# Queries, row maxima and stored heads on one PSUM bank: moving the transposes to other units of the attention

## The chip, the cores and the metric

One Trainium2 chip, one core. The metric is the device time of one execution in microseconds (us), lower is better. The engines are TensorE (PE), VectorE (DVE), ScalarE (ACT), GpSimd (POOL) and SyncE (SP, which here only issues DMAs).

## The reference

A block of three parts over 2 x 1024 tokens of width 512, each with a residual: half a mixture-of-experts FFN, attention, half the same FFN again.

```python
x = x + 0.5 * ffn(layernorm(x))      # 2 shared experts, 8 routed ones of width 352, top 2
x = x + attn(layernorm(x))
x = x + 0.5 * ffn(layernorm(x))

def attn(x):                          # 16 heads of 32, 4 key/value heads, 1024 tokens a batch
    q, k, v = x @ Wq.T, x @ Wk.T, x @ Wv.T
    q, k = rope(q), rope(k)
    attn = softmax(q @ k.T * scaling)  # no mask
    return (attn @ v) @ Wo.T
```

The change touches the attention alone.

## The kernel before

`order_of_work` writes one list of items, and each engine's program walks through the same list and does its part of every item in that order; semaphores hold between the engines. So an item's place in the list is its place in every engine's queue.

**Projections.** The 16 tiles of 128 tokens are projected in the order `PROJECTED` (batch 1 first, then batch 0), one tile for each `i`, in four parts `("project", t, 0..3)`: keys and values in parts 0 and 1, queries in parts 2 and 3, into two PSUM banks (0 and 1, or 2 and 3, in turn). VectorE and GpSimd rotate the result (`rotary`, L1766 and L1768). After four tiles the turned keys (`turn_keys`, L1262, bank 6) are split into a high part by ScalarE (L1521, `early_hi`) and a low part by VectorE (L1847, `early_lo`), and SP places them with twelve DMAs into `KS` (L1046). Queries of the first two of the eight groups (a group is one key head of one batch with its four query heads) are turned in bank 7 (`MISC`; `turn_queries`, L1272) at the tiles named by `EARLY_QUERIES`, split into the same `early_hi` (L1526) and `early_lo` (L1854), and placed by twelve DMAs into `QS` (L1056). The two buffers exist once: `split_before` makes each split wait for the DMAs of the one before.

The softmax is done with the row maximum folded into the contraction: `row_max` (L1292) multiplies a tile of 128 queries with all 1024 keys into a pair of PSUM banks, VectorE takes the negated maximum (L1859, `nmf_first` or `nmf_later`), and when a head's eight are there `place_max` turns them in `MISC` (L1300), ScalarE and VectorE split them (L1535, L1865, `place_low`), and SP writes them as two rows of `QS`. The 32 maxima of the first group stand beside the projections of the tiles `i` = 9 to 15, and use one pair of banks (4 and 5), so each matmul pair waits for the reduction before it.

**Heads.** Each group has 32 units: head `h`, half `hf` of the queries, and pair of key tiles (`pair`, 0 to 3). `un` is the unit within its group. A unit `u` has on TensorE the scores (L1310, two matmuls), half of the values of unit `u - 5` (L1325, L1326), a row maximum of the next group, and the other half of the values, eight matmuls; three pairs of banks go round. ScalarE takes the exponential (L1547, `PT`) and most high parts (L1556, `Ph`), VectorE the others (L1878); the low parts `Pl` are on GpSimd (L2017) or VectorE (L1886). Of 16 units VectorE casts 3 and subtracts 5, GpSimd subtracts 11. After each fourth unit ScalarE copies the output (L1564, `OT`), and at pair 1 `store_head` turns it in `MISC` (L1336) and VectorE normalises it with four small instructions (L1786 to L1793), the last of which, `qtok`, frees `MISC`. At `un` 5 and 21 `turn_queries` turns half of the queries of the group after next, also in `MISC`, after `store_head` of the same unit; at pair 2 of every eighth unit `place_max` uses it too.

Of the kernel before, what the change touches and what calls it, by code (L numbers as in the profile page):

```python
# [35 lines left out]
REP = NH // NKV  # L36
QT = S // P
# [139 lines left out]
UNITS = 2 * REP * (QT // 2)  # L177


def unit(u):  # L180

    n, un = divmod(u, UNITS)
    return n, un // QT, un // (QT // 2) % 2, un % (QT // 2)
# [10 lines left out]
def lo_on_vector(u):  # L194
    return u % 4 != 0 if in_last_group(u) else u % 16 in (2, 4, 8, 10, 14)
# [15 lines left out]

QUERY_STACK, KEY_STACK = (0, 1, 0), (0, 0, 1)

EARLY_QUERIES = {5: (0, 0), 9: (0, 1), 10: (1, 0), 12: (1, 1)}


def out_bank(n, hf):
# [13 lines left out]
def order_of_work():  # L231
# [131 lines left out]
    maxima = [("row_max", 0, h, t) for t in range(QT) for h in range(REP)]  # L363

    def beside_step():
        for item in beside.pop(0) if beside else ():
            work.append(item)
            if item[0] == "norm" and item[3] == 2 + TPG:
                normed.add(item[2])

    for i, t in enumerate(PROJECTED):
        if i > 0:
            beside_step()
        tq = i - QT
        if i == QT:
            work.append(("ones",))
        if tq == 0:
            work.append(("queries_start",))
        while t // TPG not in normed:
            beside_step()  # L380
        work.append(("project", t, 0))
        if tq == 0:

            work.extend([("turn_keys", PROJECTED[i - 1]), ("place_keys", ORDER[1])])
        for h in range(REP - 1):
            if tq > 0:
                work.append(maxima.pop(0))
                if h == 2 and tq <= REP:

                    work.append(maxima.pop(0))  # L390
            if h == 1:
                beside_step()
                if i in EARLY_QUERIES:
                    work.append(("turn_queries", *EARLY_QUERIES[i]))
            work.append(("project", t, h + 1))
            if i in EARLY_QUERIES and h == 1:
                work.append(("place_queries", *EARLY_QUERIES[i]))
            if i == NT - 1 and h == REP - 2:
                for h2 in range(2):
                    work.extend([("place_max", 0, h2), ("place_low", 0, h2)])  # L400
            if i > 0 and tq != 0 and h == 1:
                work.append(("turn_keys", PROJECTED[i - 1]))
                if i % TPG == 0:
                    work.append(("place_keys", PROJECTED[i - 1] // TPG))
        if tq > 0:
            work.append(maxima.pop(0))
    work.extend([("turn_keys", PROJECTED[-1]), ("place_keys", PROJECTED[-1] // TPG)])
    for h in range(2, REP):
# [3 lines left out]
    in_flight, outputs, maxima, lows = [], [], [], []  # L412
    groups = len(KV_GROUPS)
    for u in range(groups * UNITS):
        n, h, hf, pair = unit(u)
        un = u % UNITS
        if u and un == 0 and n == groups - 1:
            work.append(("spare_bank",))
        if in_flight:
            work.append(("split_hi", in_flight[-1]))  # L420
            if not lo_on_vector(in_flight[-1]):
                work.append(("split_lo", in_flight[-1]))
        work.append(("scores", u))
        in_flight.append(u)
        if lows:
            work.append(("place_low", *lows.pop(0)))
        w = in_flight[0] if in_flight[0] == u - LAG else None

        between = w is not None and unit(w)[3] > 0 and n + 1 < groups
        if between:  # L430
            work.append(("half_values", w, 0))
        if n + 1 < groups:
            work.append(("row_max", n + 1, un // QT, un % QT))
        if maxima and pair == 2:
            lows.append(maxima.pop(0))
            work.append(("place_max", *lows[-1]))
        if n + 1 < groups and un % QT == QT - 1:
            maxima.append((n + 1, un // QT))
        if len(in_flight) > 1 and lo_on_vector(in_flight[-2]):
            work.append(("split_lo", in_flight[-2]))  # L440
        if w is not None:
            in_flight.pop(0)
            work.append(("half_values", w, 1) if between else ("values", w))
            if unit(w)[3] == QT // 2 - 1:
                outputs.append(unit(w)[:3])
        if outputs and pair == 1:
            work.append(("store_head", *outputs.pop(0)))
        if n + 2 < groups and un % (UNITS // 2) == 5:
            work.append(("turn_queries", n + 2, un // (UNITS // 2)))
        if n + 2 < groups and un % (UNITS // 2) == 6:  # L450
            work.append(("place_queries", n + 2, un // (UNITS // 2)))
        if n == groups - 1 and un % QT == 0:
            work.append(("wo", un // QT))
# [30 lines left out]
def macaron(nc, ctx, x, ffn_w, gate_w, wqkv, wo, rope, ident, triones, rconst, out):  # L484
# [202 lines left out]
    o_done, o_added = signal("o_done"), signal("o_added")  # L687

    work = order_of_work()
    dispatch_place = {t: i for i, t in enumerate(t for g in ORDER for t in group_tiles(g))}  # L690
    combines = [tuple(key) for kind, *key in work if kind == "combine"]
# [1434 lines left out]
```

## Time and profile before

| | |
|---|---|
| median of 3 runs | 1828.98 us (1827.82 to 1831.81) |
| the profiled execution | 1831.98 us, its span 1830.2 us |
| mean granted clock of TensorE | 0.968 |
| projections beside the first row maxima | about 587 to 672 us |
| heads | about 674 to 1272 us |

The span is the time from the first to the last instruction. A granted clock of 1.00 is 2.4 GHz, and the lower level is 1.2 GHz, so that a stretch at 0.86 had both.

### The profile page before, as it was taken

What the parts mean: (1) busy time and instruction counts of PE and PEld (TensorE: products, weight loads), DVE (VectorE), ACT (ScalarE), POOL (GpSimd) and SP (SyncE); (2) the same over time, 40 slices, a digit from 0 to 9 for tenths busy, and PEclk for the clock granted to TensorE, in tenths of its full rate; (3) what the DMA queues carried; (4) which work ended last, traced back from release to release, by engine and by line L of the source; (5) the groups of instructions that cost most, each with busy time, mean ns of one, the idle gap of its engine ahead of it and who ended that gap; (6) DMA issues with size and microseconds to landing.
All of it is one profiled execution on the core that took longest, in us unless ns stands there. A gap on an engine that the chain in (4) does not pass through costs nothing.

```text
span 1830.2 us, 24612 instructions
## 1 busy us (share of the span) xinstructions
PE 1661.1 (91%) x8356; PEld 1328.8 (73%) x8356; DVE 1068.1 (58%) x1786; ACT 828.1 (45%) x1148; POOL 938.5 (51%) x681
## 2 busy tenths in 40 slices
PE   6999999999976578888888888887999999999997
PEld 5888898998865455555555555554888889989985
DVE  4454322222685578999989999898645432222226
ACT  4322232232322028888888888875333122323221
POOL 3115673336533127778777887763030619550746
PEclk9999999999988889999999999999989999999998
DMA  9215543333722210100011000001210535432427
GB/s 346 78 41 199 210 179 123 125 130 113 224 93 55 53 32 19 35 19 18 19 27 27 18 18 18 1 24 48 94 52 1 215 118 200 165 131 73 177 81 241
DMA packets 65829, 175.73 MB, mean 96 GB/s; under 512 B 10544, under 2 KB 11440, under 8 KB 63152
## 3 DMA queue, kind: packets, MB, share of 16 engines
q1 hardware_dynamic: 52880, 100.48, 16.8%
q0 software_dynamic: 12832, 73.67, 11.4%
q8 instruction: 75, 1.23, 0.3%
q14 instruction: 42, 0.34, 0.1%
HBM read 102.29 MB, written 55.84 MB: 86 GB/s over the span
## 4 chain that ended last, share of the span: by engine, by line
PE 52%; DVE 28%; issue 10%; DMA 6%; ACT 2%; SPq 1%; POOL 1%; DVEq 0%; POOLq 0%; ACTq 0%
PE PS L1095 9%; PE PS L1097 9%; PE PS L1096 9%; DVE nmf_later L1859 6%; DVE Pl L1886 6%; DVE Ph L1878 5%; DVE nmf_first L1859 3%; DMA xs<-x_routed 2%; DMA xn<-x_routed 2%; PE PS L1217 2%; PE PS L1292 2%; PE PS L1222 2%; PE PS L1220 2%; PE PS L1219 2%; PE PS L1218 2%
## 5 line engine op out<-in xcount | busy, mean ns | idle before, releaser
L2017 POOL TENSOR_TENSOR Pl<-PT,Ph 128x1024 fp32r<-128x1024 f32 x162 | 429.4, 2666 | 150.0 <-ACT Ph L1556 118.4
L1547 ACT ACTIVATE PT<-PS 128x1024 f32<-128x1024 f32 x256 | 258.9, 1016 | 65.0 <-PE PS L1310 53.0
L1325 PE MATMUL PS<-Ph,V 128*65 128x512 f32 x512 | 208.5, 407 | 11.3 <-DVE Pl L1886 10.2
L1556 ACT ACTIVATE Ph<-PT 128x1024 fp32r<-128x1024 f32 x198 | 208.8, 1054 | 3.1
L1859 DVE TENSOR_REDUCE nmf_later<-PS 128x1 f32<-128x1024 f32 x160 | 190.1, 1212 | 32.8 <-PE PS L1292 32.5
L1326 PE MATMUL PS<-Pl,V 128*65 128x512 f32 x512 | 203.5, 397 | 0.0
L1292 PE MATMUL PS<-KS,QS 96*128 96x512 f32 x512 | 170.0, 414 | 32.2 <-DVE nmf_first L1859 25.1
L1935 POOL TENSOR_TENSOR W<-raw,W 128x544 fp32r<-128x544 f32 x144 | 190.2, 1356 | 1.5
L1310 PE MATMUL PS<-QS,KS 98*128 98x512 f32 x512 | 174.8, 423 | 16.7 <-DVE nmf_later L1859 12.2
L1826 DVE TENSOR_TENSOR thid<-thid,PS 128x352 f32<-128x352 f32 x78 | 40.7, 521 | 245.8 <-ACT thid L1491 245.8
L1491 ACT ACTIVATE thid<-PS 128x352 f32<-128x352 f32 x78 | 36.3, 465 | 260.3 <-PE PS L1222 260.3
L1095 PE MATMUL PS<-xh,W 128*128 128x512 f32 x352 | 146.3, 416 | 3.2 <-DVE xl L1579 1.6
L1292 PEld LDWEIGHTS PS<-KS,QS 96*128 96x128 f32 x512 | 97.6, 196 | 70.1 <-DVE nmf_first L1859 32.0
L1096 PE MATMUL PS<-xl,W 128*128 128x512 f32 x352 | 142.5, 405 | 0.0
L1097 PE MATMUL PS<-xh,W 128*128 128x512 f32 x352 | 142.5, 405 | 0.0
L1923 POOL DMA_DIRECT2D raw<-ffn_w x18 | 10.0, 556 | 257.9 <-POOLq L1921 193.6
L1859 DVE TENSOR_REDUCE nmf_first<-PS 128x1 f32<-128x1024 f32 x96 | 115.1, 1215 | 36.3 <-PE PS L1292 36.1
L1310 PEld LDWEIGHTS PS<-QS,KS 98*128 98x128 f32 x512 | 91.2, 195 | 58.4 <-DVE nmf_later L1859 23.4
L1886 DVE TENSOR_TENSOR Pl<-PT,Ph 128x1024 fp32r<-128x1024 f32 x94 | 128.3, 1371 | 0.6
L1964 POOL DMA_INDIRECT x_routed<-xq,pos x64 | 64.8, 1013 | 122.2 <-issue 117.1
L1830 DVE TENSOR_TENSOR htl<-PS,hth 128x384 fp32r<-128x384 f32 x78 | 43.5, 558 | 138.8 <-ACT hth L1497 138.8
L1951 POOL TENSOR_TENSOR W<-raw,W 128x512 fp32r<-128x512 f32 (+1 forms) x36 | 43.6, 1240 | 137.2 <-ACT W L1455 137.2
(183 smaller groups left out, 4050.9 us busy)
## 6 DMA issues: line engine op xcount, KB each, us to landing
raw<-ffn_w POOLq DMA_DIRECT2D x18, 2176.0 KB, 10.4
y_routed<-ytile SPq DMA_DIRECT2D x78, 256.0 KB, 2.0
xn<-x_routed SPq DMA_DIRECT2D x40, 256.0 KB, 3.0
x_routed<-xq SPq DMA_DIRECT2D x1, 9984.0 KB, 28.8
xs<-x_routed SPq DMA_DIRECT2D x38, 256.0 KB, 3.2
QS<-later_hi SPq DMA_DIRECT2D x96, 64.0 KB, 2.0
raw<-ffn_w SPq DMA_DIRECT2D x6, 768.0 KB, 9.8
raw<-ffn_w SPq DMA_DIRECT2D x2, 2176.0 KB, 9.2
```

The costliest lines, as they stand in the source:

```text
L1095: e.matmul(dst, lh, rh, start=first, stop=False)
L1096: e.matmul(dst, lh, rl, start=False, stop=False)
L1097: return e.matmul(dst, ll, rh, start=False, stop=end)
L1292: mm = e.matmul(PS[:, i + hf, :], QS[n % 3][0:STK, h, t * P:(t + 1) * P], KS[0:STK, b, g, hf * GRP:(hf + 1) * GRP], start=True, stop=True)
L1310: mm = e.matmul(PS[:, i + j, :], KS[0:ROWS, b, g, kt * P:(kt + 1) * P], QS[n % 3][0:ROWS, h, hf * GRP:(hf + 1) * GRP], start=True, stop=True)
L1325: e.matmul(PS[0:VCOL, ob, :], V[:, b * QT + kt, g, :], high_part(u)[:, js], start=kt == 0, stop=False)
L1326: mm = e.matmul(PS[0:VCOL, ob, :], V[:, b * QT + kt, g, :], low_part(u)[:, js], start=False, stop=kt == QT - 1)
L1547: e.activation(PT[:, u % PTBUF, :], PS[:, i:i + 2, :].rearrange("p b n -> p (b n)"), ACT.Exp, scale=SCALE).then_inc(p_ready.sem, 1)
L1556: e.activation(high_part(u)[:], PT[:, u % PTBUF, :], ACT.Copy).then_inc(ph_act.sem, 1)
L1859: e.tensor_reduce(row_maxima(n)[:, h, t:t + 1], PS[:, i:i + 2, :].rearrange("p b n -> p (b n)"), AX.X, ALU.max, negate=True).then_inc(max_ ...
L1886: e.tensor_tensor(low_part(u)[:], PT[:, u % PTBUF, :], high_part(u)[:], ALU.subtract).then_inc(pl_dve.sem, 1)
L2017: e.tensor_tensor(low_part(u)[:], PT[:, u % PTBUF, :], high_part(u)[:], ALU.subtract).then_inc(pl_pool.sem, 1)
```

## The change

Three numbers in the heads, and two in the projections. The queries of the groups from the third on are turned at `un` 6 and 22 (and split and placed at 7 and 23) instead of 5 and 21 (6 and 22). The row maxima are turned at pair 3 instead of pair 2. In the projections the last two of the four early query halves go from the tiles `i` = 10 and 12 to 11 and 14; the first row maximum stands ahead of part 3 of tile `i` = 9 instead of ahead of part 1, so tile 9 has two instead of five, and the tiles 10, 11 and 12 have six instead of five.

```diff
-EARLY_QUERIES = {5: (0, 0), 9: (0, 1), 10: (1, 0), 12: (1, 1)}
+EARLY_QUERIES = {5: (0, 0), 9: (0, 1), 11: (1, 0), 14: (1, 1)}
+
+FIRST_MAXIMA = QT + 1
...
         for h in range(REP - 1):
-            if tq > 0:
+            if i > FIRST_MAXIMA or i == FIRST_MAXIMA and h == 2:
                 work.append(maxima.pop(0))
-                if h == 2 and tq <= REP:
+                if h % 2 == 0 and FIRST_MAXIMA < i <= FIRST_MAXIMA + 3:
 
                     work.append(maxima.pop(0))
...
-        if tq > 0:
+        if i >= FIRST_MAXIMA:
             work.append(maxima.pop(0))
...
-        if maxima and pair == 2:
+        if maxima and pair == 3:
             lows.append(maxima.pop(0))
             work.append(("place_max", *lows[-1]))
...
-        if n + 2 < groups and un % (UNITS // 2) == 5:
+        if n + 2 < groups and un % (UNITS // 2) == 6:
             work.append(("turn_queries", n + 2, un // (UNITS // 2)))
-        if n + 2 < groups and un % (UNITS // 2) == 6:
+        if n + 2 < groups and un % (UNITS // 2) == 7:
             work.append(("place_queries", n + 2, un // (UNITS // 2)))
```

## Rows read from the trace of the kernel before

**Rows 1.** The page, part 1: busy us, share of span, instructions, by engine.

```profile
PE 1661.1 (91%) x8356; PEld 1328.8 (73%) x8356; DVE 1068.1 (58%) x1786; ACT 828.1 (45%) x1148; POOL 938.5 (51%) x681
```

**Rows 2.** VectorE in order of time, projections: start, length, what [idle before].

```profile
591.66 0.69 DVE L1854 TENSOR_TENSOR early_lo<-PS,early_hi 128x512 fp32r<-128x512 f32 x1 [0.26 <-ACT early_hi L1526]
...
617.08 1.23 DVE L1859 TENSOR_REDUCE nmf_first<-PS 128x1 f32<-128x1024 f32 x1 [1.88 <-PE PS L1292]
...
654.95 1.22 DVE L1859 TENSOR_REDUCE nmf_first<-PS 128x1 f32<-128x1024 f32 x1 [0.83 <-PE PS L1292]
...
656.99 1.23 DVE L1859 TENSOR_REDUCE nmf_first<-PS 128x1 f32<-128x1024 f32 x1 [0.23 <-PE PS L1292]
```

**Rows 3.** Windows by tile: length, then busy us (instructions) by engine, clock, DMA.

```profile
587.60:598.30 10.70, 9.35 (x38) 7.11 (x36) 7.45 (x10) 0.88 (x2) 0.45 (x1) 0.78 0.20 48
598.30:609.40 11.10, 8.07 (x41) 5.99 (x39) 8.47 (x12) 0.88 (x2) 1.72 (x2) 1.00 0.26 64
609.40:621.70 12.30, 9.26 (x37) 6.69 (x36) 7.97 (x11) 0.28 (x1) 1.72 (x2) 0.86 0.12 30
621.70:644.20 22.50, 9.80 (x40) 7.49 (x39) 9.13 (x14) 1.48 (x3) 1.72 (x2) 0.77 0.24 58
644.20:652.90 8.70, 7.12 (x36) 5.38 (x34) 6.67 (x10) 0.28 (x1) 1.72 (x2) 1.00 0.13 32
...
661.60:671.40 9.80, 6.63 (x32) 4.68 (x30) 7.12 (x12) 0.81 (x3) 2.65 (x3) 1.00 0.00 0
```

**Rows 4.** Waits, 575 to 680 us: who waits <- for whom: total, times, longest.

```profile
ACT early_hi L1521 <- DMA QS<-early_hi: 9.8, 1, 9.8
...
PE PS L1292 <- DMA KS<-early_lo: 6.3, 1, 6.3
```

**Rows 5.** Windows, half a group of the heads each, groups 3 and 6 (counted from 0).

```profile
901.30:938.90 37.60, 32.61 (x152) 21.79 (x151) 34.23 (x44) 31.67 (x37) 29.15 (x12) 1.00 0.09 22
...
1126.90:1164.00 37.10, 33.83 (x148) 22.33 (x147) 34.46 (x43) 31.30 (x36) 29.02 (x12) 0.95 0.01 2
```

**Rows 6.** VectorE in order of time, heads of group 3.

```profile
916.65 1.23 DVE L1859 TENSOR_REDUCE nmf_later<-PS 128x1 f32<-128x1024 f32 x1 [2.16 <-PE PS L1292]
...
927.91 1.23 DVE L1859 TENSOR_REDUCE nmf_later<-PS 128x1 f32<-128x1024 f32 x1 [0.90 <-PE PS L1292]
```

**Rows 7.** TensorE in order of time, heads of group 3.

```profile
911.63 0.41 PE L1336 MATMUL PS<-identf,OT 65*128 65x65 f32 x4
914.55 0.66 PE L1272 MATMUL PS<-identf,qtok 128*128 128x128 f32 x4 [2.50 <-DVE qtok L1793]
...
925.74 0.27 PE L1300 MATMUL PS<-identf,nmf_later 128*8 128x128 f32 x1 [1.39 <-DVE qtok L1793]
```

**Rows 8.** Waits in the heads, 690 to 1130 us.

```profile
PE PS L1272 <- DVE qtok L1793: 27.6, 11, 2.5
...
PE PS L1300 <- DVE qtok L1793: 15.9, 12, 1.4
```

**Rows 9.** ScalarE in order of time, tile twelve.

```profile
626.25 0.60 ACT L1526 ACTIVATE early_hi<-PS 128x512 fp32r<-128x512 f32 x1 [1.49 <-PE PS L1272]
636.66 0.60 ACT L1521 ACTIVATE early_hi<-PS 128x512 fp32r<-128x512 f32 x1 [9.81 <-DMA QS<-early_hi]
```

**Rows 10.** The chain that ended last, in order of time: start, length, what.

```profile
634.59 1.99 DMA QS<-early_hi
```

**Rows 11.** By source line: count, ns min/median/max (casts, VectorE's and GpSimd's low parts).

```profile
L1878 DVE CAST Ph<-PT x58: 676/2070/2901, 680.2 to 1268.1; 128x1024 fp32r<-128x1024 f32 x58
L1886 DVE TENSOR_TENSOR Pl<-PT,Ph x94: 1202/1224/3404, 684.1 to 1268.8; 128x1024 fp32r<-128x1024 f32 x94
L2017 POOL TENSOR_TENSOR Pl<-PT,Ph x162: 2356/2407/3444, 679.0 to 1259.8; 128x1024 fp32r<-128x1024 f32 x162
```

**Rows 12.** VectorE in order of time, heads of group 6.

```profile
1152.58 1.23 DVE L1859 TENSOR_REDUCE nmf_later<-PS 128x1 f32<-128x1024 f32 x1 [2.37 <-PE PS L1292]
1153.72 3.02 DVE L1886 TENSOR_TENSOR Pl<-PT,Ph 128x1024 fp32r<-128x1024 f32 x1
```

## Prediction

> **What bounds the kernel now.** I read first the page's shares [rows 1]: TensorE is busy 91% of the span and VectorE 58%, but these are means over stages. The change touches two stages only, so I asked for each what its row maxima wait for: the projections from tile nine on (about 587 to 672 us), and the heads (about 674 to 1272 us).
>
> In the projections each of the 32 row maxima of the first group goes through one pair of PSUM banks: two matmuls, VectorE's reduction, then the next two matmuls. Two reductions in a row start 2.04 us apart [rows 2] (654.95 to 656.99) even with half a projection's matmuls between them, so TensorE's projection work is hidden there and the chain of 32 maxima sets the end. Stretches cut at the last reduction of each projected tile [rows 3] show: with four maxima a tile takes 8.7 us, with five 11.1 us, the last tile 9.8 us (it also turns two rows of maxima). One tile takes 22.5 us. The waits [rows 4] say why: ScalarE stood 9.8 us before the keys' high part until a DMA out of `early_hi` had landed. Turned queries and turned keys share `early_hi` and `early_lo`; in this tile both are placed, back to back. The same waits show 6.3 us in which TensorE stood before the first maximum until the keys' last DMA had landed.
>
> In the heads I looked at VectorE's order of time over half a group (16 units of group 3, counted from 0). It is busy 34.23 of 37.6 us, TensorE 32.61, ScalarE 31.67 [rows 5]: VectorE is nearly gapless, so it is the bound, and what is worth anything is its own idle time. There are two gaps of note, 2.16 and 0.90 us before a row maximum [rows 6], 3.06 us together. Both follow a TensorE wait for bank MISC [rows 7]: turning the queries comes right after turning a stored head (911.63) and waits 2.50 us for VectorE's last read of that head; the transposed maxima wait 1.39 us for the same. The waits over the steady part [rows 8] count 11 of the one and 12 of the other.
>
> **The change, part by part.** No instruction is added or removed; all are moved.
>
> *Tile nine's first maxima.* Before, TensorE stood at the first maximum with three quarters of the tile still to project. Now the second and third part and the first group's second query half come first. The keys land when they did, so the first reduction stays at 587.6 us or so; ScalarE's copy of the queries' high part must wait for the same landing (it overwrites `early_hi`), and VectorE's low part, with the first reduction queued behind it, ends 1.3 us after it by 0.60 us [rows 9] and 0.69 us [rows 2], also at about 587.6. So nothing is gained or lost at the start; the work moved into the wait is work the chain would have hidden anyway.
>
> *The chain from there.* Before: 10.7 + 11.1 + 12.3 + 22.5 + 8.7 + 8.7 + 9.8 = 83.8 us, by tile [rows 3]. After, tile nine has two maxima, the next three have six each, the last three four. First pitch: 3.1 us, that of a pair with half a projection between at the low clock (at 617.08, 1.88 of idle behind a reduction of 1.22 [rows 2]), as TensorE has just stood still. A tile of four costs 8.7 = 4 x 2.04 + 0.55; one of six 6 x 2.04 + 0.55 = 12.8, three of them 38.4. Turning queries adds about 0.35 (11.1 less 5 x 2.04 + 0.55), and falls on tiles 11 and 14, placing the keys in tile 12 about 0.3 (between 0 and VectorE's 0.69). The last three: 8.7 + 8.7 + 9.8 = 27.2. Sum 3.1 + 38.4 + 0.35 + 0.3 + 0.35 + 27.2 = 69.7. One spell at the low clock such as tile 11 had (12.3 against 10.75 for five maxima without turning) adds 1.5: 71.2. **First term: 83.8 - 71.2 = 12.6 us.** Bounds: 14.1 without that spell; -0.9 if the three tiles of six run wholly at 1.2 GHz (below).
>
> Does the 9.8 us wait return elsewhere? From one high part to the free buffer took 10.4 us (626.25 to 636.66 [rows 9]): SP issues twelve transfers, and the last one landed 1.99 us after its issue began [rows 10]. Queries of tile 11 and keys of tile 12 are now 12.8 us apart, queries of tile 14 and the last keys some 13 us (8.7 plus most of a tile). Both clear it by about 2.4 us. The queries' second half of group 1 is first read at the fifth unit of the heads, long after its landing.
>
> *The heads: maxima turned one unit later.* TensorE then reaches the transpose about 1.9 us later (eight matmuls of a unit, out of 152 in 32.61 us [rows 5]), after the 1.39 us are over. The gap of 0.90 goes. Their first reader is the next group or the eighth unit on, so lateness costs nothing; behind it on ScalarE stand the next exponential and high part, which no longer wait for the transpose.
>
> *The queries turned one unit later.* TensorE now does unit six's matmuls (1.9 us) in the 2.50 us, then still waits for the same VectorE read until 914.55, turns, and delivers the next maximum 2.1 us later, at 916.65 as before. VectorE meanwhile has one reduction it did not have, 1.23 us [rows 6]. So 2.16 - 1.23 = 0.93 us of idle is left and 1.23 saved. Together 2.13 us of 3.06.
>
> *What the saved idle time meets.* VectorE's casts took 0.68 to 2.90 us and its subtractions 1.20 to 3.40 [rows 11]: the long ones wait behind a GpSimd subtraction. Group 6, which turns no queries, shows it: VectorE busy 34.46 of 37.1 us though 0.68 us of work is gone (with 34.23 before), 0.91 us more waiting, one subtraction of 3.02 us among it [rows 12]. I take 0.3 of the 0.91, as the new order keeps more slack than that group's: 1.8 us per half group. 11 x 1.8 = 19.8; the first half, with no wait at its queries, 0.9; group 6's two halves lose a gap of 2.37 us each [rows 12], less 0.3: 4.1. **Second term: 24.8 us.** Bounds: 11 x 3.06 + 0.9 + 4.7 = 39; and about 8 (rival B).
>
> The Trainium skill (SBUF — State Buffer, section on the two separate sides) says that VectorE and GpSimd take a shared pair of ports as an exclusive lock, held for a whole instruction, for VectorE operations with two SBUF inputs or a two-port mode. The trace agrees: the shortest cast is 0.68 us and the median 2.07.
>
> The profiled execution took 1832.0 us, 3.0 more than the median 1829.0. 1832.0 - 12.6 - 24.8 = 1794.6, so against the median **1792 us**.
>
> **Rivals.** *A, the forecast:* both terms, 1785 to 1800.
>
> *B, the ports are the bound.* By the shortest durations [rows 11] a half group holds 3 x 0.68 + 5 x 1.20 + 11 x 2.36 = 34.0 us of work that excludes one another. If this can't be packed closer than in group 6 (37.1 us without any turning, only 0.4 to 0.5 us shorter than the others), a half group gains 0.5: 11 x 0.5 + 2.5 = 8 us. Then 1829 - 12.6 - 8 = 1808. For it: group 6. Against: that half had a low clock (0.95) and the 1.7 us wait for MISC that the change removes.
>
> *C, the clock.* Granted clock 0.86 in tile 11, which had no long wait, 0.77 in tiles 9 and 12 [rows 3]. Tiles of six maxima give TensorE less to do per us than those of five. At 1.2 GHz two pitches a tile grow by 1.1 (3.1 against 2.04) to 1.5 and the others by about 0.5: 5 us a tile, 15 for three, so the first term is -0.9 and the time 1829 + 0.9 - 24.8 = 1805.
>
> *D, slower.* The clock in the heads: over a half group TensorE's 32.6 us would be about 65 at 1.2 GHz, 29 more than 36. From 37/29 = 1.3 half groups (some 85 us at the low clock) on, the whole gain is gone; at three, 1829 + 50 = 1879. For it: a drop in group 6 (0.95). Against: 1.00 over the steady half, with both waits in it, and the change takes waits away.
>
> *E, all gaps close:* 39 + 14.1 = 53, 1776 us.
>
> **How the numbers follow.** A 0.59, B 0.19, C 0.11, E 0.06, D 0.03, and 0.02 that a wait I don't see cancels it all. A alone: 1785 to 1800. B and C lie at 1808 and 1805, so the range runs from 1781 to 1812 and leaves out E, D and the edges of B. A measurement tells about 0.2% (3.7 us) from no change: faster 0.95, within it 0.02, slower 0.03.
>
> **What would show it.** The last reduction before the heads near 659 instead of 671.5; no 9.8 us wait at the keys' high part; one tile no longer at 22.5 us but three at about 12.8. In the heads, TensorE's wait before the queries' turning 0.6 us instead of 2.5, none before the maxima, a VectorE gap near 0.9 after the queries, half groups of 35.8 us. Wrong if ScalarE waits for a landing at the keys of tile 12 or at the end, if casts and subtractions on VectorE grow, or if the clock row falls.

## The result, and the profile of the changed kernel

| | before | changed |
|---|---|---|
| median of four runs each, one chip (us) | 1830.39 (1827.82 to 1835.89) | 1779.12 (1774.1 to 1787.51) |
| profiled execution: time; span (us) | 1832.0; 1830.2 | 1774.1; 1772.3 |

The ratio is 0.9721, 95% interval [0.9676, 0.9765]: 51 us gained where 37 were forecast, and 1779.1 lies 2 us below the range. The sign was right, both mechanisms were at work, and the second term was far too small.

The page first, part 1 (busy us, share of the span, instructions), against [rows 1]: the counts are the same, VectorE is busy 12.4 us less, GpSimd 8.5 us less. No instruction was removed, so some instructions became shorter.

```profile
PE 1659.6 (94%) x8356; PEld 1327.1 (75%) x8356; DVE 1055.7 (60%) x1786; ACT 824.1 (46%) x1148; POOL 930.0 (52%) x681
```

**The projections.** Stretches of the changed kernel cut at the last reduction of each tile, as in [rows 3]; the first window runs from the first to the second reduction (length, busy us of PE, PEld, DVE, ACT and POOL, granted clock, DMA share, GB/s):

```profile
588.12:591.88 3.76, 3.76 (x11) 2.98 (x11) 2.43 (x4) 0.00 (x0) 0.00 (x0) 0.50 0.29 70
591.88:605.57 13.69, 10.47 (x42) 7.59 (x40) 9.23 (x12) 0.28 (x1) 1.76 (x2) 0.85 0.16 40
605.57:619.70 14.13, 10.23 (x43) 7.48 (x41) 10.01 (x13) 0.88 (x2) 1.72 (x2) 0.88 0.13 33
619.70:634.10 14.40, 9.87 (x39) 7.06 (x37) 9.83 (x14) 0.88 (x2) 1.71 (x2) 0.88 0.20 48
634.10:642.84 8.74, 6.99 (x35) 5.30 (x33) 6.69 (x11) 0.28 (x1) 1.72 (x2) 1.00 0.21 51
642.84:651.90 9.06, 7.34 (x39) 5.69 (x37) 7.28 (x11) 0.88 (x2) 1.72 (x2) 1.00 0.09 23
651.90:661.76 9.86, 6.67 (x32) 4.68 (x30) 7.16 (x12) 0.81 (x3) 2.69 (x3) 1.00 0.24 59
```

The tile of 22.5 us is gone. The chain from first to last reduction takes 73.64 us where it took 83.8: 10.2 us gained, against 12.6 in the first term. It starts at 588.12, where 587.6 was forecast. This is one trace. Eleven kernels of the experiments have the same projections, and in the twelve traces together the chain takes 73.5 to 73.7 us seven times (mean granted clock of that stretch 0.90) and 74.9, 75.7, 77.5, 77.5 and 79.9 us in the others (0.92, 0.86, 0.84, 0.84 and 0.82). The old order takes 83.6 to 84.3 us in five traces (0.86 to 0.89), so the change of order is worth 4 to 10 us there, and most of the spread goes with the clock. ScalarE's high parts in order of time show where the 9.81 us of [rows 9] went: nowhere. They stand 15.2 us apart, and the keys' (628.22) waits for TensorE, not for a DMA. The queries' of tile 14 (647.36) and the last keys' (661.83) stand 14.5 us apart and wait for TensorE too.

```profile
586.84 0.60 ACT L1528 ACTIVATE early_hi<-PS 128x512 fp32r<-128x512 f32 x1 [5.18 <-DMA KS<-early_lo]
613.05 0.60 ACT L1528 ACTIVATE early_hi<-PS 128x512 fp32r<-128x512 f32 x1 [1.95 <-PE PS L1274]
628.22 0.60 ACT L1523 ACTIVATE early_hi<-PS 128x512 fp32r<-128x512 f32 x1 [2.61 <-PE PS L1264]
```

**The heads.** From the last reduction of the projections to the last of the heads the changed kernel takes 484.1 us (661.76 to 1145.9), the kernel before 527.3 (671.45 to 1198.8): 43.2 us gained, against 24.8 in the second term. Two half groups, a steady one and one of group 6, to be held against [rows 5]:

```profile
735.95:770.36 34.41, 32.77 (x151) 21.64 (x150) 33.11 (x44) 31.37 (x37) 28.35 (x12) 1.00 0.10 24
1080.15:1114.26 34.11, 32.50 (x148) 21.32 (x147) 33.84 (x43) 30.90 (x36) 29.93 (x12) 1.00 0.01 2
```

A steady half group fell from 37.6 to 34.4 us, 3.2 us, where 1.8 were forecast. The idle time of VectorE fell from 3.37 (37.60 less 34.23) to 1.30, by 2.07; the forecast had 2.13. But its busy time, with the same instructions, fell too, from 34.23 to 33.11, by 1.1 us, where a growth of 0.3 had been put in. VectorE in order of time in that half group shows the rest:

```profile
738.99 2.08 DVE L1880 CAST Ph<-PT 128x1024 fp32r<-128x1024 f32 x1
...
749.04 1.21 DVE L1861 TENSOR_REDUCE nmf_later<-PS 128x1 f32<-128x1024 f32 x1
751.28 1.22 DVE L1861 TENSOR_REDUCE nmf_later<-PS 128x1 f32<-128x1024 f32 x1 [1.03 <-PE PS L1294]
752.42 0.68 DVE L1856 TENSOR_TENSOR later_lo<-PS,later_hi 128x512 fp32r<-128x512 f32 x1
753.02 0.68 DVE L1880 CAST Ph<-PT 128x1024 fp32r<-128x1024 f32 x1
...
765.02 1.75 DVE L1880 CAST Ph<-PT 128x1024 fp32r<-128x1024 f32 x1
```

There is one gap, 1.03 us behind the queries' turning (0.93 forecast), and none behind the maxima. The three casts of a half group take 2.08, 0.68 and 1.75 us, 4.51 together; before they took 2.09, 1.55 and 2.07 (904.49, 919.65 and 933.37 us of its trace), 5.71. Casts are one size, 0.68 us at the shortest [rows 11], so the rest is waiting, and these 1.2 us are the fall in busy time. GpSimd in order of time shows behind what (2.36 us is the shortest of its subtractions): the first cast starts while the second of a pair is under way, which ends at 740.52, and ends 0.55 us after it; the second cast falls between two of them, and the later one waits for it.

```profile
734.77 5.75 POOL L2019 TENSOR_TENSOR Pl<-PT,Ph 128x1024 fp32r<-128x1024 f32 x2
...
748.03 4.77 POOL L2019 TENSOR_TENSOR Pl<-PT,Ph 128x1024 fp32r<-128x1024 f32 x2 [1.17 <-ACT Ph L1558]
753.78 2.41 POOL L2019 TENSOR_TENSOR Pl<-PT,Ph 128x1024 fp32r<-128x1024 f32 x1 [0.98 <-DVE Ph L1880]
```

The same in VectorE's groups by line, of the changed kernel and then of the one before:

```profile
L1880 DVE CAST Ph<-PT 128x1024 fp32r<-128x1024 f32 x58 | 91.0, 1570 | 0.0
```

```profile
L1878 DVE CAST Ph<-PT 128x1024 fp32r<-128x1024 f32 x58 | 101.1, 1743 | 0.0
```

TensorE now waits 0.77 us before it turns the queries (0.6 forecast; [rows 7] had 2.50), and the waits from 680 to 1100 us hold eleven of these (second line below) and none before the maxima, where [rows 8] had twelve:

```profile
DVE nmf_later L1861 <- PE PS L1294: 8.5, 9, 1.1
PE PS L1274 <- DVE qtok L1795: 8.3, 11, 0.8
```

**The sum.** The spans differ by 57.9 us: 10.2 in the projections, 43.2 in the heads, 5.0 after the last reduction, less 0.5 because the chain began later. Of what comes after the last reduction the change moves only the last turning of maxima. That part takes 626.4 us here and 631.5 in the kernel before, and from 626.4 to 634.5 in the traces of all kernels of this document, so the 5.0 us are a part of this pair of executions, not of the change (the medians differ by 51).

### The profile page after: what moved, and what is told of

It reads as the page before. It is cut to its first block, busy times and chain, and to the rows that moved or that the text cites. A ratio compares the mean times of both kernels' runs of the same rounds, so it can differ in the third digit from the quotient of the medians.

```text
span 1772.3 us, 24612 instructions
## 1 busy us (share of the span) xinstructions
PE 1659.6 (94%) x8356; PEld 1327.1 (75%) x8356; DVE 1055.7 (60%) x1786; ACT 824.1 (46%) x1148; POOL 930.0 (52%) x681
## 4 chain that ended last, share of the span: by engine, by line
PE 56%; DVE 26%; DMA 7%; issue 6%; ACT 3%; SPq 1%; POOL 0%; DVEq 0%; ACTq 0%; POOLq 0%
PE PS L1097 10%; PE PS L1099 10%; PE PS L1098 10%; DVE nmf_later L1861 6%; DVE Pl L1888 5%; DVE Ph L1880 4%; DVE nmf_first L1861 4%; PE PS L1219 2%; DMA xn<-x_routed 2%; PE PS L1224 2%; PE PS L1222 2%; PE PS L1221 2%; PE PS L1223 2%; PE PS L1220 2%; PE PS L1294 2%
## 5 line engine op out<-in xcount | busy, mean ns | idle before, releaser
L2019 POOL TENSOR_TENSOR Pl<-PT,Ph 128x1024 fp32r<-128x1024 f32 x162 | 422.5, 2625 | 111.7 <-ACT Ph L1558 81.3
```

The source lines that it names most:

```text
L2019: e.tensor_tensor(low_part(u)[:], PT[:, u % PTBUF, :], high_part(u)[:], ALU.subtract).then_inc(pl_pool.sem, 1)
```

## The experiments

All kernels here, the control included, have two more register operations than the changed kernel (a shifted value and a clamped one are kept in registers of their own). `changed` is the changed kernel with nothing else: 1783.17 us (1775.84 to 1789.58), ratio 0.9733 [0.9704, 0.9761], half groups 34.43 us. Ratios are to the kernel before on the same chip, in five rounds; `low_four`, `casts_two`, `before_low_four` and the three `pe_` kernels had three.

### One part of the change at a time

The kernel before with one part each. `proj_only` has the first three pieces of the diff, with `QT + 1` written out for `FIRST_MAXIMA`; of these only the first is shown:

```
-EARLY_QUERIES = {5: (0, 0), 9: (0, 1), 10: (1, 0), 12: (1, 1)}
+EARLY_QUERIES = {5: (0, 0), 9: (0, 1), 11: (1, 0), 14: (1, 1)}
```

`maxima_only` has the first line below, `queries_only` the other two, `heads_only` all three:

```
-        if maxima and pair == 2:
+        if maxima and pair == 3:
-        if n + 2 < groups and un % (UNITS // 2) == 5:    (turn_queries)
+        if n + 2 < groups and un % (UNITS // 2) == 6:
-        if n + 2 < groups and un % (UNITS // 2) == 6:    (place_queries)
+        if n + 2 < groups and un % (UNITS // 2) == 7:
```

> The kernel before with the projections' part of the change alone: early queries at tiles 11 and 14, the first row maximum ahead of part 3 of tile nine, six maxima in tiles 10 to 12; the heads stay as before. Theory: the stretch from the first to the last reduction goes from 83.8 to 73.6 us as in the changed kernel, and nothing else moves: 10 us less in all, ratio 0.9945, half groups in the heads still 37.6 us. Rival: the heads' half groups lock into another pattern with another start, and the time is off the 10 us by more than 5 in either direction.

> The kernel before with the heads' part of the change alone (queries turned at units 6 and 22, maxima at pair 3); the projections stay as before, with the 9.8 us wait. Theory: half groups of 34.4 us instead of 37.6, the heads some 42 us shorter, ratio 0.977. Rival: the shorter half group needs the start that the new projections give, and the half groups are at 35.5 us or more here, 25 us less in all.

> The kernel before with the queries turned one unit later and nothing else; the maxima are still turned at pair 2. Theory: of the changed kernel's 3.2 us a half group, 1.1 come from VectorE's idle time at the queries, and 1.1 from waits behind GpSimd which the new place of the cast after the queries saves; both belong to this move: half groups of 35.4 us, some 25 us less in all, ratio 0.986, the shortest of the three casts near 0.68 us. Rival: the fall of the GpSimd waits belongs to the maxima's move or to both together: half groups of 36.5 us, 13 us less.

> The kernel before with the maxima turned at pair 3 instead of 2 and nothing else; the queries stay at units 5 and 21. Theory: only the 0.9 us gap of VectorE goes, half groups of 36.7 us, and group 6 loses its two gaps of 2.4 us: 10 plus 5, some 15 us less, ratio 0.992. Rival (the GpSimd waits fall here): half groups of 35.6 us, some 28 us less. Second rival (VectorE's waits behind GpSimd take the place of the gap): half groups still 37.6 us and 5 us less.

| kernel | median us | ratio | projections us | steady half group us |
|---|---|---|---|---|
| before, here | 1832.91 | | 83.8 | 37.60 |
| proj_only | 1829.62 | 0.9978 [0.9961, 0.9994] | 73.7 | 37.6 |
| heads_only | 1789.20 | 0.9752 [0.973, 0.9774] | 84.1 | 34.43 |
| queries_only | 1806.25 | 0.9843 [0.9819, 0.9867] | 84.3 | 35.46 |
| maxima_only | 1823.12 | 0.9941 [0.9919, 0.9964] | 83.6 | 37.65 |

`heads_only` gains 43.7 us, which is what the heads gave in the changed kernel's trace. From the last reduction of the projections to the last of the heads its trace has 484.1 us, as the changed kernel's, `queries_only` 500.7, `maxima_only` 519.6 and the kernel before 527.3.

In `queries_only` a half group takes 35.46 us, in `maxima_only` 37.63; a window of each, from cast to cast:

```profile
908.93:944.39 35.46, 32.60 (x152) 21.60 (x151) 33.25 (x44) 31.71 (x37) 28.92 (x11) 1.00 0.10 24
```

```profile
920.04:957.67 37.63, 34.11 (x151) 22.99 (x151) 33.25 (x45) 31.30 (x37) 28.17 (x12) 0.95 0.09 22
```

VectorE is busy 33.25 us in both, a good 1.0 us less than before, and the two moves together give 1.1. But they shorten different casts. The three of a half group take 2.08, 1.55 and 2.07 us before, 2.07, 0.68 and 2.08 in `queries_only`, 2.08, 0.68 to 0.98 and 1.55 in `maxima_only`, and 2.08, 0.68 and 1.75 in the changed kernel. So the queries' move frees the second cast and the maxima's move shortens the third. That the second is short in `maxima_only` too comes with the long gaps told below and needs no move: in the kernel before the only cast behind a long gap takes 0.94 us where the others take 1.53 to 1.58, and in `before_low_four` the ten behind long gaps take 0.68 to 1.00, the one behind a gap of 2.15 takes 1.56. First a long gap and the cast behind it in the kernel before, then the short gap of `before_low_four` and its cast:

```profile
729.27 1.23 DVE L1859 TENSOR_REDUCE nmf_later<-PS 128x1 f32<-128x1024 f32 x1 [3.61 <-PE PS L1292]
...
732.27 0.94 DVE L1878 CAST Ph<-PT 128x1024 fp32r<-128x1024 f32 x1
```

```profile
918.55 1.23 DVE L1860 TENSOR_REDUCE nmf_later<-PS 128x1 f32<-128x1024 f32 x1 [2.15 <-PE PS L1292]
...
921.55 1.56 DVE L1879 CAST Ph<-PT 128x1024 fp32r<-128x1024 f32 x1
```

What also differs is the clock. In `maxima_only` TensorE's wait before the queries is 2.67 us, and the granted clock behind it is low for a few microseconds, so that the turning takes 1.11 us instead of 0.66 and VectorE's gap is 3.66 instead of 2.16. Of that kernel, TensorE and VectorE in order of time:

```profile
951.05 1.11 PE L1272 MATMUL PS<-identf,qtok 128*128 128x128 f32 x4 [2.67 <-DVE qtok L1794]
...
954.66 1.23 DVE L1860 TENSOR_REDUCE nmf_later<-PS 128x1 f32<-128x1024 f32 x1 [3.66 <-PE PS L1292]
```

and windows of it around this place:

```profile
940.00:950.00 10.00, 7.75 (x36) 4.98 (x34) 9.93 (x14) 8.63 (x10) 8.20 (x4) 1.00 0.00 1
950.00:960.00 10.00, 8.95 (x34) 6.42 (x35) 6.11 (x11) 5.66 (x7) 6.05 (x3) 0.83 0.11 26
960.00:970.00 10.00, 9.77 (x49) 6.50 (x47) 9.64 (x15) 9.73 (x13) 6.93 (x4) 1.00 0.23 55
```

All eleven of its gaps behind the queries are of this kind, 3.2 to 3.7 us, about 1.4 more than 2.15. A spell costs less than that where the cast behind it is spared: two half groups of the kernel before with one spell take 76.0 us where two others take 75.2, and four of `proj_only` with three spells 154.4 where 150.4 would be usual. At 0.8 to 1.3 us each eleven spells are an estimated 9 to 15 us, so the maxima's move alone may well have shortened the work, and the spells have taken it back; no half group of `maxima_only` without a spell is there to show it. The length of the wait does not decide alone: behind waits of 2.5 us the kernel before has one long gap of eleven, `proj_only` three. This also tells where `proj_only`'s gain went in part. Its projections are shorter by 10 us, and its heads took 530.4 us instead of 527.3, two spells more. In its profiled execution the span is 8.2 us shorter than before (1822.0 against 1830.2), in the medians 3.3; its twelve executions have mean clocks of 0.958 to 0.969, and more such spells in those not profiled would account for the rest, which no trace here shows.

So the parts are not additive: alone the heads' two moves gain 26.7 and 9.8 us in the medians, together 43.7. The intervals are some 4 us wide to each side, so the medians alone would leave this open; the traces of the heads say it more sharply, with 26.6 and 7.7 us against 43.2. With a wait of 0.6 (`queries_only`) or 0.77 us (changed kernel) no gap of that kind is left in either trace.

### The projections: which move removes the wait

`undo_first` is the changed kernel with the first maxima in their old places, `undo_early` the one with the early queries back at tiles 10 and 12.

> The changed kernel with the first row maxima back at part 1 of tile nine and five in tiles 9 to 12, the early queries still at tiles 11 and 14. Theory: the early queries' move alone takes away the 9.8 us wait, the chain of 32 maxima is as long either way: first to last reduction 74 to 76 us against 73.6, up to 2 us more in all (TensorE's work at the low clock in tile nine). Rival: the maxima's move is what gives the queries of tile 11 and the keys of tile 12 their room: with tiles of 11.1 us instead of 12.8 ScalarE waits for a landing there, and the stretch is 80 us.

> The changed kernel with the early queries turned at their old tiles (10 and 12) and the first maxima at their new ones. By the wait theory the 9.8 us wait of ScalarE for the landing of the queries' copies is back before the keys' high part, projections of 83 us instead of 75, time 1788. Rival (the order of the maxima alone spares the wait): 1779.

`undo_first`: 1778.47 us, 0.9694 [0.9669, 0.9719], projections 74.8 us. `undo_early`: 1789.36 us, 0.9772 [0.9754, 0.979], projections 87.1 us, and the wait is back, as ScalarE's last row in tile twelve shows:

```profile
634.34 0.60 ACT L1522 ACTIVATE early_hi<-PS 128x512 fp32r<-128x512 f32 x1 [9.74 <-DMA QS<-early_hi]
```

The early queries' move carries the whole gain of the projections. With the first maxima's move alone they take 3 us longer in the one trace (87.1 against 83.8), at a granted clock of 0.82 where the kernel before had 0.89, so the clock may be the reason. Beside the other, with 73.5 to 79.9 us in the traces of the changed order and 74.8 here, its worth can't be told from nothing.

### The heads: gap against wait

`cast_6` moves a cast of VectorE from unit 7 to 6 of 16, `queries_78` turns and places the queries one unit later still (7 and 8).

> The changed kernel with VectorE's cast of unit 7 given to ScalarE and that of unit 6 to VectorE; the queries stay at units 6 and 7. Theory (the extra gain over the forecast is that the cast after the queries falls into GpSimd's gap): the cast now stands ahead of the turned queries' low part, GpSimd is in a subtraction then, the cast takes 1.5 to 2.1 us again, and half groups grow from 34.4 to 35.2 us or more, some 10 us in all. Rival (VectorE's waits behind GpSimd are the same in sum wherever the casts stand, and it was the shorter idle time alone): half groups stay at 34.4 us within 0.2.

> The changed kernel with the queries turned one unit later again (units 7 and 23, placed at 8 and 24). Theory: TensorE's last wait for the bank (0.77 us) and VectorE's gap of 1.0 us behind it go; with the waits behind GpSimd as they are, half groups of 33.4 us and 12 us less than the changed kernel. Rival: the cast after the queries leaves GpSimd's gap, 1.1 us come back, and the time is that of the changed kernel or 3 us more. Second rival: the next stored head, at unit 9, now waits for the queries' low part, and the wait has only moved.

`cast_6`: 1778.26 us, 0.9702 [0.9677, 0.9726], half groups 34.25 us. `queries_78`: 1785.12 us, 0.9747 [0.9719, 0.9775], half groups 34.55. A half group of each:

```profile
920.00:954.25 34.25, 32.69 (x152) 21.65 (x151) 33.19 (x44) 30.95 (x37) 28.20 (x11) 1.00 0.10 24
```

```profile
957.00:991.55 34.55, 32.68 (x152) 21.71 (x151) 34.28 (x44) 31.42 (x37) 29.52 (x12) 1.00 0.10 24
```

In `cast_6` the theory that a moved cast would meet a subtraction and cost 0.8 us or more misses: its three casts take 2.08, 0.81 and 1.55 us, 4.44 together as in the changed kernel (4.51), and its rival (the same sum of waits, the same length within 0.2 us) holds. `queries_78` is the telling one. VectorE has no gap of note left and is busy 34.28 us of 34.55, 1.2 more than in the changed kernel, with casts of 2.08, 2.08 and 1.90. Yet a half group is longer by only 0.1 us: the idle time has become waiting behind GpSimd, and TensorE's next stored head waits in its turn. VectorE, then TensorE, in order of time:

```profile
991.61 2.09 DVE L1881 CAST Ph<-PT 128x1024 fp32r<-128x1024 f32 x1
...
995.48 0.46 PE L1338 MATMUL PS<-identf,OT 65*128 65x65 f32 x4 [0.73 <-DVE later_lo L1857]
```

While VectorE stands for TensorE, GpSimd gets on with its subtraction, and the cast behind the gap no longer meets it: here a gap of VectorE and a wait behind GpSimd trade one for the other. What then keeps the length near 34.4 us is not shown by either kernel.

### What bounds a half group now

My next theory was that the ports which the two engines share are the bound: 34.0 us by rival B's sum, against 34.1 to 34.55 in all these kernels. Four kernels change where casts and subtractions run, the last beside the old order:

```
low_six          u % 16 in (2, 4, 8, 10, 12, 14)   subtractions on VectorE, before: (2, 4, 8, 10, 14)
low_four         u % 16 in (2, 4, 8, 14)
casts_two        u % 16 in (1, 13)                 casts on VectorE, before: (1, 7, 13)
before_low_four  low_four's edit in the kernel before
```

> The changed kernel with VectorE doing six low parts of 16 units instead of five (unit 12 too), GpSimd ten. Theory (port theory: after the change a half group is bound by what VectorE and GpSimd can't do at once, 3 x 0.68 + 5 x 1.20 + 11 x 2.36 = 34.0 us, and only 0.4 us of 34.4 are free of it): the sum is now 32.8, VectorE's own work 31.5, so half groups shrink to 33.2 us, some 16 us less than the changed kernel. Rival (VectorE theory: VectorE's own work and its gaps are the bound, the waits behind GpSimd are an accident of phase): half groups grow by about 1 us to 35.4 us.

> The changed kernel with four low parts on VectorE instead of five (unit 10 goes to GpSimd, which has twelve). Port theory: 3 x 0.68 + 4 x 1.20 + 12 x 2.36 = 35.2 us, half groups of 35.4 us, 14 us more than the changed kernel. VectorE theory: VectorE has 1.1 us less to do, half groups of 33.3 to 34.4 us.

> The changed kernel with two casts on VectorE instead of three; the high part of unit 7 goes to ScalarE. Port theory: 34.0 less 0.68 is 33.3 us, half groups of 33.7 us if ScalarE (31.3 us busy, 32.4 then) keeps up, 10 us less. VectorE theory: VectorE loses 0.68 us of work, and half groups the same 0.7 us; the two theories differ in the 1.7 to 2.1 us that the other casts take: they stay so long by the port theory, and by the other they may fall. Rival: ScalarE, now with an exponential and a high part in three units in a row, becomes late and half groups are 34.4 us or more.

> The kernel before with four low parts on VectorE instead of five (unit 10 goes to GpSimd). Port theory: before the change the 34.0 us of exclusive work left 3.6 of 37.6 us free, so 1.2 more fits: half groups stay within 0.5 of 37.6 us, or shrink since VectorE has 1.1 us less to do, and what costs 14 us after the change costs nothing before it. Rival: it costs the same before as after, 1 us a half group and 14 us in all, and the port was the bound of both.

Medians and ratios: `low_six` 1779.81, 0.9711 [0.969, 0.9732]; `low_four` 1786.16, 0.975 [0.9733, 0.9767]; `casts_two` 1773.64, 0.9682 [0.9657, 0.9708]; `before_low_four` 1834.94, 1.002 [1.0009, 1.0032]. One half group of each of the first three:

```profile
925.19:959.66 34.47, 32.75 (x152) 21.64 (x151) 33.17 (x46) 31.43 (x37) 25.98 (x10) 1.00 0.10 24
```

```profile
925.48:960.42 34.94, 32.75 (x152) 21.65 (x151) 32.60 (x43) 31.41 (x37) 30.50 (x12) 1.00 0.10 23
```

```profile
938.94:973.16 34.22, 32.59 (x152) 21.63 (x151) 32.45 (x43) 32.03 (x38) 28.17 (x12) 1.00 0.10 24
```

The theory falls. `low_six` takes 1.2 us of work off the ports (a subtraction of 2.36 us on GpSimd becomes one of 1.20 on VectorE) and the half group stays at 34.47, not 33.2: VectorE has 1.2 us more to do and waits 1.1 less, a cast of 1.75 being 0.68 now. `low_four` was to take 35.4 and takes 34.94, which is under its own sum of 35.2 (4 x 1.20 + 12 x 2.36 + 3 x 0.68). The sum of shortest lengths is no hard floor: recorded instructions overlap (the reduction at 751.28 above lasts 1.22 and the next begins 1.14 later), so each of its seven VectorE instructions counts about 0.08 us too much. Less that, an estimate, the sum is 34.6, below 34.94, and `low_four` alone would leave the ports as a bound of its own longer half group; it is `low_six` that speaks against them in the changed kernel. `before_low_four` is inconclusive: its half groups take 38.2 to 38.8 us, save one of 36.7; its casts are shorter (mean 1596 ns, not 1743), and ten of its eleven gaps behind the queries are over 2.9 us and the clock of its heads from 680 to 1120 us is 0.94 where the kernel before has 0.99.

Then each of the engines alone. `pe_less` leaves out the low part's value products of units 5 and 9, `pe_more` adds them twice, `ve_less` takes one row maximum in eight over half of the keys:

```
 for j in tiles:
-    e.matmul(... high_part(u)[:, js], start=kt == 0, stop=False)
+    mm = e.matmul(... high_part(u)[:, js], start=kt == 0, stop=False)
+    if u % 16 in (5, 9):
+        continue                                   pe_less
```

```
+width = 1 if n > 0 and t == 5 else 2               ve_less
-e.tensor_reduce(..., PS[:, i:i + 2, :] ...)
+e.tensor_reduce(..., PS[:, i:i + width, :] ...)
```

> Leaves out part of the computation: the two low-part value products of units 5 and 9 of every 16, four 512-column matmuls per half group, which take 0.235 us each in TensorE's back-to-back stretches, 0.94 us together. Nothing of VectorE's or GpSimd's changes. TensorE theory (after the change TensorE is busy 32.8 of 34.4 us and stands only 0.77 us behind the queries, 0.6 behind a row maximum and 0.1 behind ScalarE, so its work is the bound): half groups of 33.5 us, 13 half groups and the last group, about 14 us less than the changed kernel's 1779 to 1783, 1767. Port theory (the 34.0 us that VectorE and GpSimd can't overlap are the bound): half groups 34.0 to 34.4, 1774 to 1783.

> Changes the computation: the low-part value products of units 5 and 9 of every 16 are added twice, four more matmuls per half group, 0.94 us of TensorE. TensorE theory: half groups 35.3 us, about 14 us more than the changed kernel, 1795. Port or VectorE theory: TensorE has 1.6 us of idle per half group to take it, half groups stay at 34.4 to 34.7, 1779 to 1786.

> The same four matmuls left out, and one more subtraction (unit 12 of 16) on VectorE, which lowers the exclusive port work from 34.0 to 32.8 us per half group. If TensorE's work comes first and the ports stop it at 34.0 in the kernel without this second edit, this one gives 33.5 or less and the other 34.0. TensorE alone: both 33.5. Ports alone: 33.2, and the other stays at 34.4.

> Leaves out part of the computation: from group 1 on, the row maximum of one tile of each head is taken over the first 512 keys alone, two reductions per half group of 512 columns instead of 1024, about 0.53 us shorter each (1.20 less the 0.68 that VectorE's other 128x512 reading of PSUM takes), 1.07 us per half group. They touch no port shared with GpSimd, and TensorE's work stays. VectorE theory (its own order is the bound, 33.1 us of work and waits plus 1.3 of idle): half groups 33.4 us, 1766 to 1770. Rival (VectorE comes earlier to GpSimd's subtractions and waits that much longer for them): casts of 1.75 and 0.68 us grow to 2.1 or so, half groups 34.1 to 34.4, 1777 to 1783.

| kernel | what is changed per half group | window us | median us (rounds) |
|---|---|---|---|
| changed | nothing | 34.4 | 1783.17 (5) |
| pe_less | TensorE 0.94 less | 34.40 | 1777.95 (3) |
| pe_less_low_six | and the ports 1.2 less, VectorE 1.2 more | 34.44 | 1775.54 (3) |
| pe_more | TensorE 0.94 more | 34.72 | 1785.10 (3) |
| ve_less | VectorE 1.06 less | 34.17 | 1778.70 (5) |

The windows of `pe_less`, of `pe_more` and of `ve_less`:

```profile
928.92:963.32 34.40, 32.29 (x148) 20.98 (x147) 33.10 (x45) 31.40 (x37) 28.34 (x11) 1.00 0.10 24
```

```profile
928.34:963.06 34.72, 33.34 (x156) 22.26 (x155) 33.24 (x45) 31.48 (x37) 28.64 (x11) 1.00 0.10 24
```

```profile
927.37:961.54 34.17, 32.79 (x152) 21.63 (x151) 32.38 (x45) 31.39 (x37) 28.31 (x12) 1.00 0.10 24
```

Each of them was to shorten (or lengthen) the half group by about 1 us under the theory that its engine is the bound; none does by more than 0.3. (TensorE's 0.94 us is four matmuls at the 0.235 us at which they follow each other; its recorded busy time changes by some 0.5, as the records overlap.) What is taken from one engine comes back as its wait for another. In `pe_less`, TensorE's waits for VectorE's row maxima double; the waits from 820 to 1060 us, first of `pe_less`, then of the control:

```profile
PE PS L1274 <- DVE qtok L1798: 5.3, 7, 0.8
PE PS L1312 <- DVE nmf_later L1864: 4.8, 8, 0.6
```

```profile
PE PS L1274 <- DVE qtok L1796: 5.3, 7, 0.8
PE PS L1312 <- DVE nmf_later L1862: 2.4, 4, 0.6
```

and in `ve_less`, VectorE gains a wait for the stored heads that it did not have:

```profile
DVE nmf_later L1863 <- PE PS L1294: 4.1, 4, 1.0
DVE rL L1789 <- PE PS L1338: 3.5, 7, 0.5
```

The lengths of `pe_less`, `pe_more` and `ve_less` are those of their rivals, though in `ve_less` the casts did not grow as its rival had it (0.68 and 1.73 us as in the control); `pe_less_low_six`, at 34.44, fits none of its three forecasts. Among TensorE's work, VectorE's work and the ports no single bound of the changed half group is found: TensorE's 32.8 us of work, VectorE's 33.1 of work and waits behind GpSimd, and the pair's sum near 34 all lie within 1.6 us of its 34.4. That they hold it in turn along its 16 units fits this, but no run shows it.

### The two small gains together

`best` is `undo_first` with `casts_two`'s edit.

> The changed kernel with two casts per half group on VectorE (not three) and the first row maxima back in their old place. If the two gains seen apart (1773.64 for the casts, 1778.47 for the maxima, against 1779 to 1783 for the changed kernel) add: 1770. If both are only scatter of the clock: 1775 to 1783.

It gave 1775.21 us, ratio 0.9691 [0.9666, 0.9716], half groups 34.23: no better than either alone, whose intervals overlap with it and, in part, with that of the control. Two casts on VectorE instead of three shorten the half group by 0.2 us, 14 x 0.2 = 2.8 us; what goes beyond that in the medians can't be told from scatter. No version beats the changed kernel by more than some 0.5%.

## Why the prediction was right and wrong

**The start of the chain.** Right: 588.12 us against 587.6, nothing gained or lost (the first reductions of all traces here lie between 585.0 and 590.3, so the half microsecond says nothing).

**The first term, 12.6 us.** The mechanism was right: the wait for the landing is gone and comes back nowhere, since both pairs of high parts clear it. The size was 10.2. Three pieces were short: the first pitch was 3.76, not 3.1 (its window stands at 0.50, wholly at the lower level of 1.2 GHz); the three tiles of six maxima took 13.69, 14.13 and 14.40, 42.2 together where 40.6 stood in the sum with its one low spell. The windows show 0.85 to 0.88 in all three. This is rival C in small: low spells in each of the three tiles, but 1.7 us beyond the forecast in this trace, not 15, and some 4 to 6 us more than this in the three slowest traces of this order (77.5 to 79.9 us). The last three tiles took 27.66 against 27.55.

**The maxima in the heads.** Right: no wait is left and their gap is gone.

**The queries in the heads.** Right: 0.77 us of wait against 0.6, a gap of 1.03 against 0.93. The idle time fell by 2.07 us per half group against 2.13. The 1.9 us of TensorE's work behind both figures doesn't follow from its own source (eight matmuls out of 152 in 32.61 us are 1.7); with 1.7 the wait comes to 0.8, which is what was measured.

**What the saved idle time meets.** This is the step that failed. It said "I take 0.3 of the 0.91" as growth of VectorE's waits behind GpSimd; in the trace and in the one-part kernels they shrank, by 1.1 us per half group. The error was to read group 6, whose casts and subtractions fall elsewhere and whose half group held a clock of 0.95, as the rule for the others. A wait behind GpSimd went here not with the amount of work but with where each cast falls beside a subtraction. Three casts decide it, and they went from 2.09, 1.55 and 2.07 to 2.08, 0.68 and 1.75. That it is the casts was measured; that they had to fall so well could not be read from shares, and I don't have a run that predicts it from the order alone.

Behind this stands a wider error: the forecast took VectorE for the bound ("nearly gapless, so it is the bound") and added its idle time and its waits behind GpSimd as two terms that don't know of each other. `queries_78` has 1.55 us more of such waits than the changed kernel and no gap, and its half groups are as long within 0.1 us; `ve_less` takes 1.06 us of VectorE's work away and gains 0.26. So the short casts are where the trace books the gain, and a half group comes to 34.25 (`cast_6`), 34.43 or 34.55 us (`queries_78`) whether its three casts take 4.4 us or 6.1. What sets that length stays open.

In the sum: 11 half groups at 3.17 instead of 1.8 are 15.1 us more, the first half (1.5 against 0.9) and group 6's two (about 6 against 4.1) some 2.5 more: 24.8 + 15.1 + 2.5 = 42.4 of the measured 43.2. The one low spell in the kernel before is the rest within the rounding of these lengths.

**Rival B, the ports as bound at 1808.** Wrong as forecast, since a half group gained 3.2 us and not 0.5. Its figure of 34.0 came close to the new length, which led me to take it for the floor afterwards; `low_six` says that it isn't, with 34.47 us where the sum was 32.8. The Trainium skill (SBUF — State Buffer, section on the two separate sides) says that whichever of the two engines starts first keeps the shared pair for the whole instruction and that the other fully blocks. The trace agrees: a cast that takes 0.68 us alone takes 2.08 and ends 0.55 us after the subtraction under way (738.99 above). A length of the half group doesn't follow from it, as `low_six` shows.

**Rival C and D, the clock.** In the heads the clock did the opposite of D: all gaps of the changed kernel are short, and the kernel before has one long one (3.61 us at 729.27), which the second term did not hold. C's price was right only in kind.

**Rival E, 1776.** The time is near the measured one for a reason that was not E's: 1.3 us of idle remain per half group, and the projections gave 10.2 and not 14.1.

## What to carry to other kernels

When an operation is moved by one unit, count the gap that it leaves and also which instructions of a contending engine the neighbours will then meet; take the growth or fall of such waits from both signs, here plus or minus 1 us in 37, do not add the two as if they were independent, and multiply by the number of repetitions before the range is written. If a stage's engines are all within a few per cent of its length, work taken from one comes back as a wait for another: 1 us of it bought 0 to 0.3 us here, so look for orders of work and not for less work. And test the parts alone and together, because 27 and 10 us made 44.

## What was not expected of the hardware

The same wait of TensorE is followed now by a low clock, now not. Behind some 2.5 us of it the granted clock stayed at 1.00 ten times of eleven in the kernel before, and once in eleven in `before_low_four`; behind 2.67 us it fell each time in `maxima_only`. When it fell, VectorE's gap behind it grew from 2.15 us to between 2.96 and 3.77. Removing a wait of that length was therefore worth more here than its own idle time. The number of such spells may be a part of the kernel before's scatter, which no trace shows, as one execution of each kernel was profiled. What decides on a spell the runs leave open.

The Trainium skill (SBUF — State Buffer, section on the two separate sides) speaks of full blocking; the trace adds that the blocked engine's row in the profile is a longer instruction (a cast of 2.08 us for one of 0.68), and not idle time, so that VectorE's busy share overstates its work: 12 us of it vanished here with no instruction less.
